# Router logits carried as extra columns of the value and output projections, and a reordered tile

## The reference

```
x = x + retention(layernorm(x)) @ Wo        # 8 heads of 16, chunks of 64, decay gamma per head
n = layernorm(x)
probs = softmax(n @ Wg)                      # 8 experts
top_w, top_i = top_k(probs, 2);  top_w /= sum(top_w) + 1e-8
x = x + sum_e combine[e] * (relu(n @ W1[e])**2 @ W2[e])    # hidden 256 per expert
```

## Time and profile before

| what | value |
|---|---|
| median of three runs | 287.58 us |
| the profiled execution | 287.56 us |
| its span in the profile | 285.8 us |
| TensorE matmul busy | 272.0 us (95%), 3662 instructions |
| VectorE busy | 219.2 us (77%), 569 instructions |
| ScalarE busy | 182.7 us (64%), 265 instructions |
| GpSimd busy | 205.3 us (72%), 165 instructions |
| TensorE's granted clock | 0.999 of full speed |

### The profile page before, as it was taken

How to read it: one execution, slowest core, us unless ns; L and a number is a source line. 1 busy time by engine, 2 the same in 40 slices (tenths; PEclk the granted TensorE clock), 3 DMA queues, 4 the chain that set the end, 5 groups by cost and what they waited for, 6 DMA issues and landing times.

```text
span 285.8 us, 8944 instructions
## 1 busy us (share of the span) xinstructions
PE 272.0 (95%) x3662; PEld 214.0 (75%) x3662; DVE 219.2 (77%) x569; ACT 182.7 (64%) x265; POOL 205.3 (72%) x165
## 2 busy tenths in 40 slices
PE   7979859799999999999999999999999999999995
PEld 6566538568887788777887788777887788878883
DVE  3749848996769965996769965896859768998783
ACT  2354569466873697556964687556965567686861
POOL 2114888878969698669968699579968668566452
PEclk9999999999999999999999999999999999999999
DMA  7429043213250251304450250203420252043201
GB/s 233 128 60 304 7 189 100 84 31 124 76 148 2 78 186 48 103 5 136 126 147 2 79 175 15 71 5 108 153 76 2 77 158 90 17 141 119 76 0 73
DMA packets 13577, 26.80 MB, mean 94 GB/s; under 512 B 1120, under 2 KB 6624, under 8 KB 13536
## 3 DMA queue, kind: packets, MB, share of 16 engines
q1 hardware_dynamic: 13536, 26.23, 28.5%
HBM read 24.00 MB, written 2.23 MB: 92 GB/s over the span
## 4 chain that ended last, share of the span: by engine, by line
PE 56%; POOL 17%; issue 15%; DVE 5%; DMA 2%; ACT 2%; POOLq 1%; DVEq 0%
POOL act_lo L1067 14%; PE h_ps L338 7%; PE y_ps L353 6%; PE h_ps L340 6%; PE h_ps L339 6%; PE y_ps L359 6%; PE y_ps L354 6%; PE bank L485 3%; POOL rstd L1021 2%; PE bank L507 2%; PE bank L418 2%; PE bank L497 2%; DMA scale<-scratch 1%; PE bank L450 1%; PE y_ps L317 1%
## 5 line engine op out<-in xcount | busy, mean ns | idle before, releaser
L1067 POOL TENSOR_TENSOR act_lo<-act_f,act_hi 128x512 fp32r<-128x512 f32 x112 | 145.6, 1324 | 46.0 <-ACT act_f L955 45.9
L765 DVE SCALAR_TENSOR_TENSOR act_s<-h_ps,scale 128x1024 f32<-128x1024 f32 x64 | 77.9, 1218 | 29.6 <-PE h_ps L340 13.5
L950 ACT ACTIVATE act_hi<-act_s 128x1024 fp32r<-128x1024 f32 x64 | 67.8, 1059 | 29.7 <-DVE act_s L765 29.5
L955 ACT ACTIVATE act_f<-act_s 128x1024 f32<-128x1024 f32 x64 | 66.8, 1044 | 0.0
L338 PE MATMUL h_ps<-x_hi,w_lo 128*128 128x512 f32 x128 | 53.9, 421 | 1.7 <-DVE attn L658 1.7
L353 PE MATMUL y_ps<-act_hi,w_lo 128*128 128x512 f32 x128 | 53.8, 421 | 0.0
L340 PE MATMUL h_ps<-x_hi,w_hi 128*128 128x512 f32 x128 | 50.6, 395 | 0.0
L339 PE MATMUL h_ps<-x_lo,w_hi 128*128 128x512 f32 x128 | 50.4, 394 | 0.0
L354 PE MATMUL y_ps<-act_hi,w_hi 128*128 128x512 f32 x128 | 50.2, 392 | 0.0
L359 PE MATMUL y_ps<-act_lo,w_hi 128*128 128x512 f32 x128 | 40.4, 396 | 0.1
L1021 POOL TENSOR_TENSOR rstd<-variance,minus_half 128x4 f32<-128x4 f32 x16 | 18.4, 1152 | 19.5 <-DVE variance L622 19.4
(11 more groups left out here) (123 smaller groups left out, 387.8 us busy)
## 6 DMA issues: line engine op xcount, KB each, us to landing
scale<-scratch SPq DMA_DIRECT2D x32, 512.0 KB, 4.0
x_t_in<-x_tr SPq DMA_DIRECT2D x8, 256.0 KB, 4.9
x_all<-x SPq DMA_DIRECT2D x8, 256.0 KB, 4.8
out<-out_sb SPq DMA_DIRECT2D x8, 256.0 KB, 4.1
scale<-w SPq DMA_DIRECT2D x1, 768.0 KB, 4.7
cst<-constants SPq DMA_DIRECT2D x1, 417.0 KB, 4.8
cst<-constants SPq DMA_DIRECT2D x1, 256.0 KB, 2.8
scale<-w SPq DMA_DIRECT2D x1, 256.0 KB, 5.6
```

Source lines behind the costliest of these rows:

```text
L765: nc.vector.scalar_tensor_tensor(out=act_s[:, u % 2], in0=h_ps[:, u % 2], scalar=0.0, in1=scale[:, f % 2, e].unsqueeze(1).to_broadcast([P, ...
L950: nc.scalar.activation(act_hi[:, u % 4], act_s[:, u % 2], ACT.Square).then_inc(act_hi_ready, 1)
L955: nc.scalar.activation(act_f[:, u % 2], act_s[:, u % 2], ACT.Square).then_inc(act_f_ready, 1)
L1067: nc.gpsimd.tensor_tensor(act_lo[:, u % 4, n], act_f[:, u % 2, n], act_hi[:, u % 4, n].bitcast(F32), ALU.subtract).then_inc(pool_low_ready, 1)
```

## The change

The router's logits are no longer a product of their own. A token's new x is its old x plus rstd times (o @ Wo), so its logits are (old x) @ Wg plus rstd times o @ (Wo @ Wg), with Wg centered. `project_v` has 8 more columns that give (old x) @ Wg; ScalarE's `copy_v` puts them beside x (`x_all` becomes 136 wide). `project_out` has 8 more columns with Wo @ Wg, which `route_outputs` computes once, and `add_attention` adds both on 136 columns. Since 4 x 136 columns don't fit a bank, group 3 of both projections goes to another bank (`v_place`, `out_place`). `route` is gone. The ranking (`rank_experts`, `mark_chosen`) works on the raw logits, `shift_logits` subtracts the best from the sorted eight in SBUF, the root is taken as exp(half the logit) times (denominator times variance)**-0.5, so GpSimd's power is on 4 columns (`root_denominators`) and the reciprocal on VectorE is gone.

q and k of tile 2 are three rounded products too, so the split of w_q and w_k and of x^T of tile 2 moves ahead of the loop. The order of the queues changes: in the loop k comes in slot 1, q in slot 3, transpose_k in slot 4, project_v in slot 5; ScalarE copies k, then high_x, then masks q; VectorE decays k before q; in the start the roots of tile 0 are transposed ahead of w1_product(0, 0), and GpSimd takes the root's power ahead of all low pieces.

```diff
@@ -365,58 +372,61 @@ tensor
+            def route_outputs():
+                pe.wait_ge(second_loaded, DMA)
+                pe.wait_ge(v_z_ready, 1)
+                pe.matmul(y_ps[:, 0:EXPERTS], cst[:, C_WO_T:C_WO_T + P], w_g, start=True, stop=True).then_inc(wog_done, 1)
...
+            def project_q(s):
...
+                else:
+                    pe.wait_ge(x2_ready, s)
+                project(s, 0, q_bank(s), q_done)
+            def project_k(s):
...
+                elif s >= 2:
                     pe.wait_ge(root_t_ready, s - 1)
+                    pe.wait_ge(attn_ready, PAIRS * s)
...
             def project_v(s):
                 if s == 1:
-                    pe.wait_ge(attn_ready, 3)
+                    pe.wait_ge(attn_ready, PAIRS)
                 elif s >= 2:
                     pe.wait_ge(q_m_ready, s + 1)
                     pe.wait_ge(q_d_ready, s + 1)
+                    pe.wait_ge(x_hi_ready, s)
...
                 for g in range(GROUPS):
-                    last = pe.matmul(v_bank(s)[:, P * g:P * (g + 1)], x_t_in[:, s % XT_RING, P * g:P * (g + 1)],
-                                     w_center[:, 2], start=True, stop=True)
+                    last = pe.matmul(v_place(s, g), x_t_in[:, s % XT_RING, P * g:P * (g + 1)], w_vg, start=True, stop=True)
@@ project_out
-                    last = pe.matmul(bank1[:, P * g:P * (g + 1)], o_t[:, s % 2, g], w_out, start=True, stop=True)
+                    last = pe.matmul(out_place(g), o_t[:, s % 2, g], w_out, start=True, stop=True)
@@ slot
-                    if n == 5:
-                        route(p)
...
                     if n == 1:
-                        project_qk(a)
+                        project_k(a)
                     if n == 3:
+                        project_q(a)
+                    if n == 4:
                         transpose_k(a)
-                    if n == 4:
+                    if n == 5:
                         project_v(a)
@@ start
             center_piece(1)
-            route(0)
             state_updates(1)
             center_piece(2)
             center_piece(3)
+            center_piece(4)
+            transpose_roots(0)
             w1_product(0, 0)
-            center_piece(4)
             outputs_within(1, (0, 1))
-            transpose_roots(0)
             w1_product(0, 1)
@@ vector
+            def rank_experts(s):
+                raw = x_all[:, s % X_RING, :, P:WIDE]
+                dve.wait_ge(x2_ready, s + 1)
+                for g in range(GROUPS):
+                    last = nc.vector.max(best[:, g], raw[:, g])
...
             def shift_logits(s):
...
-                    last = nc.vector.tensor_scalar(logits[:, g], l_ps[:, g], top[:, g:g + 1],
+                    last = nc.vector.tensor_scalar(shifted[:, g], best[:, g], best[:, g, 0:1],
                                                    rstd[:, 1, s % STAT_RING, g:g + 1], ALU.subtract, ALU.mult)
...
+            def weigh(s):
+                nc.vector.tensor_reduce(total[:], expd[:], AX_X, ALU.add).then_inc(weigh_step, 1)
+                nc.vector.scalar_tensor_tensor(out=denom[:, 0], in0=total[:], scalar=TOP_EPS, in1=expd[:, :, 0],
+                                               op0=ALU.mult, op1=ALU.add).then_inc(weigh_step, 1)
...
             def spread_roots(s):
+                nc.vector.tensor_tensor(root[:], half_expd[:], r_denom[:].unsqueeze(2).to_broadcast([P, GROUPS, TOP]),
+                                        ALU.mult).then_inc(spread_step, 1)
...
@@ vector, loop
-                if a < TILES:
-                    decay_q(a)
                 scale_h(f, 1)
                 low(u)
                 if a < TILES:
                     decay_k(a)
+                    decay_q(a)
                 scale_h(f, 2)
                 low(u + 1)
                 if p < TILES:
+                    rank_experts(p)
                     shift_logits(p)
                 scale_h(f, 3)
                 low(u + 2)
                 if p < TILES:
-                    choose(p)
+                    mark_chosen(p)
+                    weigh(p)
                 if a < TILES:
                     decay_scores(a, decay_order(a)[0:1])
                 scale_h(f, 4)
                 low(u + 3)
                 if a < TILES:
-                    decay_scores(a, decay_order(a)[1:2])
+                    decay_scores(a, decay_order(a)[1:3])
                 if p < TILES:
                     spread_roots(p)
                 if a < TILES:
-                    decay_scores(a, decay_order(a)[2:])
+                    decay_scores(a, decay_order(a)[3:])
@@ scalar, copy_v
                 for g in range(GROUPS):
+                    nc.scalar.copy(x_all[:, s % X_RING, g, P:WIDE], v_place(s, g)[:, P:WIDE])
                     last = nc.scalar.activation(v_z[:, s % 2, PAIRS * g:PAIRS * (g + 1), ::3],
@@ scalar, exponentiate
-                nc.scalar.activation(expd[:], logits[:], ACT.Exp).then_inc(expd_ready, 1)
+                nc.scalar.activation(expd[:], shifted[:], ACT.Exp)
+                nc.scalar.activation(half_expd[:], shifted[:, :, 0:TOP], ACT.Exp, scale=0.5).then_inc(expd_ready, 1)
@@ scalar, start and loop
             copy_roots(0)
+            high_qk()
+            high_x_t(2)
             high_second()
             copy_o(1)
-            mask_q(2)
-            copy_k(2)
-            high_qk()
             for f in range(TILES):
                 square(u)
-                if f >= 1 and a < TILES:
-                    mask_q(a)
+                if a < TILES:
                     copy_k(a)
                 if p < TILES:
                     high_x(p)
+                if a < TILES:
+                    mask_q(a)
                 square(u + 1)
                 if a < TILES:
                     copy_v(a)
                 if f >= 1:
                     copy_y(f - 1)
                 square(u + 2)
@@ gpsimd, start and loop
             low_x(0)
+            root_denominators(0)
+            pool.wait_ge(combine_ready, 1)
             low_piece(1)
-            root_shares(0)
-            pool.wait_ge(combine_ready, 1)
             low_piece(2)
             low_piece(3)
             low_piece(4)
+            low_qk()
+            low_x_t(2)
             root_variance(2, 0)
             low_second()
-            low_qk()
...
+                if f == 0:
+                    root_variance(p, 1)
                 low(u)
+                if 1 <= f and p < TILES:
+                    root_variance(p, 1)
                 if p < TILES:
-                    root_variance(p, 1)
                     low_x(p)
```

More of the change, by code:

```diff
@@ L512, in transpose_x2 @@
                 for g in range(GROUPS):
[L513 removed]
+                    last = pe.transpose(bank1[:, P * g:P * (g + 1)], x_all[:, s % X_RING, g, 0:P], ident)
                 last.then_inc(t2_done, 1)
[L516 to L525 removed]
             def transpose_roots(s):
@@ L612, in statistics @@
                 for g in range(GROUPS):
[L613 removed]
+                    last = nc.vector.bn_stats(stats[:, which, r, g], xs[:, g, 0:P])
                 last.then_inc(norm_step[which], 1)
@@ L714, in choose, with weighed @@
+            def weigh(s):
+                def weighed(n):
+                    dve.wait_ge(weigh_step, WEIGH_STEPS * s + n)
                 dve.wait_ge(expd_ready, s + 1)
[L715 to L721 removed]
```

264 lines of the change are left out of this document (126 added, 138 removed).

## The result

Four runs of the changed kernel took 290.43 to 292.89 us, median 290.62; four of the kernel before had the median 287.33. The ratio is 1.0129, with an interval from 1.0075 to 1.0183: slower by about 3 us. The forecast was 287.7, its range ended at 290.4. The profiled execution is one of 290.62 us with a span of 288.7; the one before had 285.8. So 2.9 us are to be found.

What follows compares the result with a forecast made beforehand. TensorE was taken to bound the kernel after the first tile. Tiles 1 to 5 +2.0, tile 6 -0.84, start and first tile -1.0, together +0.2 on 287.56: forecast 287.7 us, range 284.0 to 290.4.

Steps and rivals of the forecast that it cites:

- the middle tiles: Tiles 1 to 5: matmuls -0.78, two waits +0.28 and +0.80, lock +0.10 us each; together +2.0 us.
- wait one: Value projection, each middle tile: it waits for VectorE's decay_q and restarts from a stop, 0.28 us.
- The rounded third tile: Start: q and k products take 1.40 instead of 1.72 us where TensorE waits anyway, worth 0.
- the matmuls saved: TensorE, middle tiles: logits group removed, 0.89 us, less 0.05 for added projection columns; net 0.78 with both projections.
- the lock: VectorE steps wait for the GpSimd instruction under way; 0.1 us a middle tile taken, 0.9 if the spread loses.
- start and first tile: Everything up to the end of the first tile: 1.0 us gained, bounds 0 and 3.7.
- w1(0,0) starts at 31.5: Start: low_piece(1) moves behind combine_ready; attention outputs follow, putting tile 1's output projection at 38.4 instead of 37.58 us.
- tile 6 -0.84: Tile 6: the logits group goes, with columns added to one projection only; 0.84 us gained.
- Rival 3: Middle tiles: the lock becomes the bound, TensorE stops before outputs_within, 0.9 us a tile; 291.7 us; chance 0.20.
- the y_t wait: First w2 product, tiles 1 to 5: TensorE stalls for ScalarE's copy_y behind copy_v, 0.8 us, between 0.6 and 1.2.
- Rival 1: Tiles 1 to 5: the stall for copy_y does not bite, 4.0 us off, 283.7 us; chance 0.25.

Runs made afterwards that it cites:

- pool_yields: middle_all with GpSimd waiting in tiles 0 to 5 for the spread of the roots between the two halves of act_lo(u+3): 286.91 us, ratio 0.9962.
- fill_start: The changed kernel with seven matmuls of zeros in two TensorE gaps at 29.5 to 31.45 us: 293.64 us, ratio 1.0209.
- shift_strided: The changed kernel with the four shifts written to every second element of a wider tile: 290.54 us, ratio 1.0114.
- rank_first_tile6: The changed kernel with rank_experts ahead of VectorE's low(u+1) in tile 6 alone: 289.47 us, ratio 1.0063.
- y_and_scores: y_first, and on VectorE the first decay_scores of a tile ahead of weigh: 291.62 us, ratio 1.0156.
- fill_more: fill_and_gate with 16 more matmuls of zeros in TensorE's gaps between 24 and 47 us: 292.09 us, ratio 1.0146.
- best_yield: pool_yields with fill_more's edits, and GpSimd waiting in tile 0 for the shifts before act_lo(1): 283.91 us, ratio 0.982.
- y_first: The changed kernel with ScalarE's copy_y ahead of copy_v in tiles 1 to 5: 290.63 us, ratio 1.0098.
- scale_gate: The changed kernel with three of tile 0's four scale transfers held back on SP until w1(0,1) is done: 292.73 us, ratio 1.0159.
- fill_and_gate: fill_start and scale_gate together, against the changed kernel: 291.55 us, ratio 1.0125.
- middle_all: y_and_scores with decay_q ahead of decay_k, and rank_experts ahead of low(u+1) in tile 6: 289.15 us, ratio 1.0056.
- start_order: The changed kernel with low_piece(1) and w1(0,0) in the start where they stood in the kernel before: 293.12 us, ratio 1.0167.

## Why the prediction was wrong

**Right: the middle tiles.** +0.40 us a tile was forecast, +0.40 measured, with the stop at L356 where it was put (0.75 for 0.80) and wait one of 0.18 (for 0.28). The rounded third tile is worth 0, as said. That the sum is exact is luck, since sizes made up for each other: the matmuls saved 0.53 us and not 0.78. From start to start in a tile of pool_yields, which has no stop, the logits group is gone (0.81 in the kernel before), the two projections cost 0.07 more, the w1 products 0.05, and the w2 products 0.17 more (12.14 for 11.97), which I have no cause for; the 0.89 was taken to the second instruction behind the group and so held a restart. And the lock cost nothing where 0.10 was taken.

**Wrong: "start and first tile", -1.0 taken, +0.33 measured.** The chain of the roots came as worked out, the first scale 1.2 us sooner still (36.37 for 37.6). The step that failed is "w1(0,0) starts at 31.5, and the attention outputs behind it (1.4+0.8+1.4+0.8+0.9 us, ...)": it took every matmul at full clock. TensorE was busy for 2.74 and 2.05 us of the two stretches of 4 us before 32 (3.55 and 2.90 in the kernel before, whose clock stayed full), and its clock fell to the half level for some 3.4 us (the windows miss 0.03 and 0.40 of 4 us, each at half speed). Up to outputs_before that is 1.3 us, by fill_start (36.12 for 37.55, its roots' transpose 0.12 sooner). That the clock falls is no bad luck: the changed kernel's four means are 0.992 or 0.993. Of the kernel before, 61 timed executions with a mean of 0.998 or more have the median 287.4 us, 21 with 0.994 or less 289.0.

The place of the fall varies, and that shows how deep the miss goes. In nine traces of kernels with the changed order of the start (the changed kernel's among them) the clock fell between 31.5 and 34.5, and the output projection of tile 1 stands 19.6 us behind that of tile 0. In three (shift_strided, rank_first_tile6, y_and_scores) it fell at 39 to 41, and the distance is 18.3, which is what the forecast worked out (38.4 less the 20.1 of tile 0's). Yet the projection of tile 2 stands 49.6 to 49.7 us behind that of tile 0 in those three, 49.4 in the changed kernel and 49.0 in the kernel before. So even with w1(0,0) as forecast the 1.0 us did not come. The rows of shift_strided show TensorE standing in the middle of that projection, in the stop behind matmul 726 (see fill_start), and the 512-column products behind it are up to 0.58 us apart, since the clock is then at half level:

```profile
37.62 0.38 PE L518 MATMUL bank<-cst,o_t 128*128 128x136 f32 x1 [1.23 <-ACT o_t L941]
38.52 1.44 PE L518 MATMUL bank<-cst,o_t 128*128 128x136 f32 x7 [0.51 <-issue]
```

fill_more shows that the clock is one of three covers, each hiding the next: the clock, the instruction packet behind the sooner scale transfers (nothing can pass the 726th matmul before 39 us there, or 38 with the gate), and GpSimd's lock on the shifts. The third had been forecast, up to 4 us of it (3.05 for the four shifts in the changed kernel, 4.65 in fill_more); the other two had not. Only best_yield, which has edits against all three, has its start ahead of the kernel before.

**Wrong: "tile 6 -0.84", +0.55 measured with tile 7.** The matmul term was right to about 0.2: with the stops gone the two tiles take 53.0 us, 0.6 or 0.7 less than before. The failed step is that no lock was priced there: -0.84 was the matmul term alone. I had followed VectorE against GpSimd through a middle tile only; in tile 6, where GpSimd's pattern is another, the shift loses its race by 0.1 us, and that costs 1.2 (rank_first_tile6).

**Rival 3 was right as a mechanism** and late by one cover: the y_t wait hid it in the middle tiles. Rival 1 took it for granted that 0.8 us a tile would come back if that wait were not there; y_first shows 0.05, and 0.93 only once VectorE's queue was reordered and GpSimd yielded (32.99 to 32.06, wait one's 0.18 in it).

## What to carry to other kernels

A stop that you can take away is worth what the next one behind it leaves: work out the second-latest answer before pricing the first. Where VectorE's small steps read two SBUF operands (or scale within SBUF) beside a GpSimd that works in long instructions, let GpSimd wait for the small step; 0.4 us there bought 0.5 of the whole tile. And work out the special tiles (first, last, the ones with another split) by themselves: both failed steps were in those.

## What the runs showed of the hardware

- TensorE stands without a wait at a fixed place, behind matmul 726 or 727 in ten kernels (0.34 to 2.26 us), and goes on 2.2 to 2.4 us behind the start of a 0.02 MB packet on the instruction queue; with two transfers of 0.5 MB ahead of it that packet starts at 36.8 to 37.0 us (fill_start, changed kernel), with one at 35.1 to 35.6 (scale_gate, fill_and_gate), with none at 33.7 (kernel before). That TensorE waits for this packet is inferred from these times. Two kernels have such a stop again behind matmul 2863 (0.92 and 0.83 us); there the last packet had started 2.3 us before in y_and_scores, but 4.0 in middle_all, so that this stop is not explained. The Trainium skill, page "Runtime: NRT & Kernel Launch", section "Instruction fetch mechanics", says that an engine refills its instructions in 16 KiB blocks through its own DMA queue, and that this is mostly hidden. The size agrees with the packets here; that it is hidden doesn't, for up to 2.26 us.
- A fall of the granted clock that was filled away at one place came back later (31.8 to 35.2 in the changed kernel, 39.2 to 46.0 in fill_start, 39.5 to 42.9 in fill_and_gate, 54.2 to 57.6 in fill_more), until in best_yield most gaps and stops up to 55 us were gone. What exactly it takes was not settled.
- A VectorE step of 0.2 us beside back-to-back GpSimd instructions takes 1.0 to 1.3, and four in a row took up to 4.81 us (start_order), about one GpSimd instruction each; writing them to every second element changed nothing.
- The start of otherwise equal kernels moved by up to 3 us (the roots' transpose at 29.02 to 32.12), so parts of the span tell such edits apart better than totals.
